# Zero fills in pieces, planes copies on ScalarE, the last row scatters ahead of the meta scatters, and doubled expert operands with a single landing buffer

## The chip, the cores and the metric

One core of a Trainium2 chip. The time is that of one execution of the program on the device, in microseconds (us), as a median of repeated runs. A profiled execution gives the trace.

## What is computed

A transformer block on x of 2048 tokens by 512, all in float32: a linear attention layer with 32 heads of 64, then a mixture of 8 experts of which each token takes 2.

```python
xn = layernorm(x)
q = relu(xn @ Wq); k = relu(xn @ Wk); v = xn @ Wv           # 512 x 2048 each, 32 heads
kv = einsum('bhsd,bhse->bhde', k, v)
out = einsum('bhsd,bhde->bhse', q, kv) / clip(q . k.sum(axis=2), 1e-6)
x = x + out @ Wo + bo
xf = layernorm(x)
scores = xf @ gate_w.T + gate_b + bias
gates = softmax(top_k(scores, 2))
h = silu(w1[e] @ xf + b1[e])                                # 352 wide
x = x + sum over the two experts e of gates * (w2[e] @ h + b2[e])
```

## The kernel before

The program is written engine by engine (SP for DMA issues, GpSimd, ScalarE, VectorE, TensorE), each with its list in program order; semaphores alone order them against each other. A matmul with near-float32 precision is made of three (function `three`): an operand is split into a high part (a cast, ScalarE) and a low part (the rest, VectorE). SBUF is laid out by hand, and many buffers share an address at different times.

**Stage K** (to about 390 us): four column chunks c of Wk, each with 16 row tiles. Chunk 0 also makes layernorm 1 and the transposes of x, and it splits Wk: `load_wk(c)` loads 1 MB into the single buffer wk_in, `split_wk` (ScalarE and VectorE) makes wk_hi and wk_lo. `WK_SPLIT` places these splits in the row tiles of chunk 0: block 1 in tiles 2 to 5, block 2 in tiles 8 to 11, block 3 in tiles 13 to 15. Chunks 1 to 3 take in four head pairs each (`load_pair`, `pe_kv`, `pe_m`), which are loaded when m of two pairs before is put. The SP list ahead of the pairs also holds `zero_rows`: xr_dram, a DRAM scratch of 137 blocks of 128 rows of 2 KB, is filled with zeros, because unused slots of an expert's last tile must read as zeros.

**Stage Q** (to about 805 us): 16 row tiles of four column blocks: project q, normalize, transpose, multiply by m. Then layernorm 2 (xn2), gate scores (`dots`, one VectorE instruction with a product into gprod for each expert), top 2 (`put_scores`). GpSimd routes: `put_mask` makes the mask of a tile from its top 2, TensorE ranks it (`rank`, held by mask_ready), VectorE adds the expert's base (`put_slot8`), `put_slots` makes two slots for each token, `put_rows` scatters the rows of xn2 to them in xr_dram (indirect DMAs, L699) and L714 scatters the token's number and score difference to meta_dram. Rows are scattered as two planes of 16 bits (low words, high words), which the copy `put_planes` (L725, GpSimd) makes in xp. The Q list of ScalarE is `act_unit` and `act_tile`: act_q, act_qsT, act_qs in each block.

**Stage W** (to about 842 us): w1 and w2 come in as raw float32, 46 steps k; TensorE transposes one (`w_transpose`), ScalarE makes the high part (`w_hi`), VectorE the low part (`w_lo`) or, for the steps in PE_STEPS, TensorE and ScalarE (`subtract_hi`, `w_act_lo`). Meanwhile GpSimd puts the last two tiles in slots and makes the table: first half meta_row (which block of xr_dram each expert tile reads), then the last row scatters and the gather of the meta rows (L809), then the second half tile_expert, then the bias columns of experts 6 and 7 (`put_b2`, L768), which w_transpose of steps 40 and on need.

**Expert stage** (to about 1022 us): 39 tiles of 128 slots. `load_tile(i)` (SP, L583) loads 128 rows with a transposing DMA into xgT; ScalarE copies the low words (`act_rec`, L1177) and VectorE the high words (`dve_rec`, L1630) into gx, the record. From gx come gT_hi (ScalarE) and gT_lo (VectorE), then h on TensorE (`pe_h`), a copy of h (ScalarE, h_in), its transposes (`pe_hT`, L2039), silu (ScalarE), hT_hi and hT_lo (VectorE), y (`pe_y`, two tiles behind h), y times the gate (`dve_y`, VectorE, L1648), and the scatter that adds y to out (`add_out`, GpSimd, L763). xgT has two buffers; gx, gT_hi, gT_lo and the PSUM banks of h and y have one each. ScalarE makes record i + 1 ahead of the copy of h of tile i.

Of the kernel before, what the change touches and what calls it, by code (L numbers as in the profile page):

```python
# [48 lines left out]
E = 8  # L49
# [8 lines left out]
MROWS = E * EROWS + 1  # L58
FAR = 1e30
# [5 lines left out]
def block_kernel(nc, x, Wq, Wk, Wv, Wo, bo, gate_w, gate_b, gbias, w1, b1, w2, b2, out):  # L65
    xnT_dram = nc.dram_tensor("xnT_dram", (NT, P, D), F32, kind="Internal").ap()
    xr_dram = nc.dram_tensor("xr_dram", (MROWS * P, 2 * D), U16, kind="Internal").ap()
# [52 lines left out]
    gprod = sb("gprod", D, 201 * KB)  # L120
# [98 lines left out]
    gT_hi = sb("gT_hi", D, 184 * KB, F32R)  # L219
    gT_lo = sb("gT_lo", D, 186 * KB, F32R)  # L220
    gx = sb("gx", D, 188 * KB)
    h_in = sb("h_in", H, 190 * KB)
    hT_hi = [sb("hT_hi0", HB * P, 190 * KB + 1408, F32R), sb("hT_hi1", HB * P, M0 + 5120, F32R)]
    hT_lo = [sb("hT_lo0", HB * P, 190 * KB + 2944, F32R), sb("hT_lo1", HB * P, 190 * KB + 4480, F32R)]
    xgT = [sb(f"xgT{b}", 2 * D, (196 + 2 * b) * KB, U16) for b in range(2)]
    y_last = sb("y_last", D, 198 * KB)
    y = sb("y", 2 * D, M0 + 1024)

    with ExitStack() as ctx:
# [131 lines left out]
        s_xt = [sem(f"s_xt{i}") for i in range(2)]  # L361
# [49 lines left out]
        y_bank = lambda i: pA[:, (i - (NS - 2)) * 512:(i - (NS - 3)) * 512] if isinstance(i, int) and i >= NS - 2 else pK[:, 512:1024]  # L411
        hT = pT[:, 0:HB * P]
        planes = lambda a: a[:, :].rearrange("p (h n) -> p h n", h=2)
        words = lambda a: a[:, :].bitcast(U16).rearrange("p (n h) -> p h n", h=2)

        @block.sync
        def _(sp):
# [29 lines left out]
            sp.dma_start(xr_dram[E * EROWS * P:MROWS * P, :].rearrange("p (h n) -> p h n", h=2),  # L447
                         zero16[:, :].unsqueeze(1).to_broadcast([P, 2, D])).then_inc(xr_zeroed, 16)
            sp.wait_ge(wk_lo_ready, 3 * FB)
            load_wk(3)  # L450
# [123 lines left out]
            sp.wait_ge(s_metain, 16)  # L574
# [3 lines left out]
            def load_tile(i):  # L578
                if i >= 2:
                    sp.wait_ge(rec_lo, i - 1)  # L580
                    sp.wait_ge(rec_hi, i - 1)
                row = sp.value_load(meta_row[i:i + 1, 0:1], min_val=0, max_val=MROWS - 1)
                sp.dma_start_transpose(xgT[i % 2][:, :].rearrange("p (c n) -> p c n", n=P),  # L583
                                       xr_dram[ds(row * P, P), :]).then_inc(s_xt[i % 2], 16)
# [13 lines left out]
        def _(pool):  # L598
# [69 lines left out]
            pool.wait_ge(xr_zeroed, 16 * (E + 1))  # L668
# [25 lines left out]
            def put_rows(r, b):  # L694
                rows = xp_last if isinstance(r, int) and r == NT - 1 else xp
# [151 lines left out]
        def _(act):  # L847
# [354 lines left out]
            def act_tile_e(i, b, e=None, last=False):  # L1202
# [3 lines left out]
                if not last:  # L1206
                    act_gT(i + 1)
# [895 lines left out]
```

## Time and profile before

| | us |
|---|---|
| median of 3 runs | 1029.01 |
| lowest and highest | 1028.38, 1030.11 |
| the profiled execution | 1029.53 |
| its span | 1027.8 |

| engine | busy us | share of the span | instructions |
|---|---|---|---|
| TensorE (PE) | 995.1 | 97% | 4863 |
| VectorE (DVE) | 736.7 | 72% | 1593 |
| ScalarE (ACT) | 543.3 | 53% | 1361 |
| GpSimd (POOL) | 266.3 | 26% | 423 |

The span is the time between the first and the last instruction; the execution takes 1.7 us more. The granted clock of TensorE is 0.99 of full speed as a mean. In the rows a timeline line is: start, length, engine, line of the kernel, operation, output from input, count, and in brackets the idle time of the engine before it and what ended it. A row of the windows is one stretch: its bounds and width, busy us (and instructions) of PE, PEld, DVE, ACT and POOL, the granted clock, the busy share of the DMA engines and what they moved in GB/s. L12 is line 12 of the kernel.

### The profile page before, as it was taken

What the parts mean: (1) busy time and instruction counts of PE and PEld (TensorE: products, weight loads), DVE (VectorE), ACT (ScalarE), POOL (GpSimd) and SP (SyncE); (2) the same over time, 40 slices, a digit from 0 to 9 for tenths busy, and PEclk for the clock granted to TensorE, in tenths of its full rate; (3) what the DMA queues carried; (4) which work ended last, traced back from release to release, by engine and by line L of the source; (5) the groups of instructions that cost most, each with busy time, mean ns of one, the idle gap of its engine ahead of it and who ended that gap; (6) DMA issues with size and microseconds to landing.
All of it is one profiled execution on the core that took longest, in us unless ns stands there. A gap on an engine that the chain in (4) does not pass through costs nothing. (4 is left out here: it accounts for less than half of the span.)

```text
span 1027.8 us, 17481 instructions
## 1 busy us (share of the span) xinstructions
PE 995.1 (97%) x4863; PEld 827.6 (81%) x4864; DVE 736.7 (72%) x1593; ACT 543.3 (53%) x1361; POOL 266.3 (26%) x423
## 2 busy tenths in 40 slices
PE   9998799999999999999899999999999979999998
PEld 7876688888888888888788887888888868888886
DVE  7876565565556567857788888888888866666665
ACT  4542544444444455865455555555555775555553
POOL 1000000000000002222644444444444752333334
PEclk9999899999999999999999999999999989999999
DMA  9999592000010011332211111111115854776873
GB/s 320 374 348 340 183 374 90 21 20 20 20 40 23 20 62 62 103 119 96 90 63 52 51 51 51 53 59 51 59 43 141 234 162 78 118 106 106 117 111 53
DMA packets 120254, 115.20 MB, mean 112 GB/s; under 512 B 47033, under 2 KB 94570, under 8 KB 120082
## 3 DMA queue, kind: packets, MB, share of 16 engines
q1 hardware_dynamic: 110962, 97.73, 31.3%
q0 software_dynamic: 9248, 16.95, 8.7%
q8 instruction: 20, 0.33, 0.1%
q14 instruction: 24, 0.20, 0.1%
HBM read 42.91 MB, written 63.35 MB: 103 GB/s over the span
## 5 line engine op out<-in xcount | busy, mean ns | idle before, releaser
L1013 ACT ACTIVATE qs<-q,nrec 128x64 f32<-128x64 f32 x512 | 129.6, 335 | 106.9 <-DVE nrec L1404 104.2
L621 POOL TENSOR_TENSOR wv_lo<-wv_in,wv_hi 128x512 fp32r<-128x512 f32 x4 | 5.2, 1292 | 417.3 <-ACT wo_hi L934 417.3
L1686 PE MATMUL pK<-wk_hi,xnT_hi 128*128 128x512 f32 (+1 forms) x256 | 101.0, 394 | 11.9 <-DVE xnT_lo L1259 11.8
L1686 PE MATMUL pA<-k_hi,xn_hi 128*128 128x512 f32 x256 | 101.0, 394 | 0.5 <-DVE k_lo L1279 0.5
L1686 PE MATMUL pK<-wq_hi,xnT_hi 128*128 128x512 f32 x256 | 100.5, 393 | 0.0
L1687 PE MATMUL pK<-wk_lo,xnT_hi 128*128 128x512 f32 (+1 forms) x256 | 100.4, 392 | 0.0
L1688 PE MATMUL pK<-wk_hi,xnT_lo 128*128 128x512 f32 (+1 forms) x256 | 100.2, 391 | 0.0
L1688 PE MATMUL pK<-wq_hi,xnT_lo 128*128 128x512 f32 x256 | 99.8, 390 | 0.0
L1688 PE MATMUL pA<-k_hi,xn_lo 128*128 128x512 f32 x256 | 99.8, 390 | 0.0
L1687 PE MATMUL pA<-k_lo,xn_hi 128*128 128x512 f32 x256 | 99.7, 389 | 0.0
L1687 PE MATMUL pK<-wq_lo,xnT_hi 128*128 128x512 f32 x256 | 99.7, 389 | 0.0
L1686 PE MATMUL pX<-m_hi,qsT_hi 128*128 128x512 f32 x240 | 99.6, 415 | 0.0
L1688 PE MATMUL pX<-m_hi,qsT_lo 128*128 128x512 f32 x240 | 94.8, 395 | 0.0
L1687 PE MATMUL pX<-m_lo,qsT_hi 128*128 128x512 f32 x240 | 94.3, 393 | 0.0
L763 POOL DMA_INDIRECT out<-y,slot_token x38 | 59.1, 1556 | 123.5 <-DMA out<-y,slot_token 85.5
L1279 DVE SCALAR_TENSOR_TENSOR k_lo<-pK,k_hi 128x512 fp32r<-128x512 f32 x64 | 44.1, 689 | 57.3 <-ACT k_hi L881 57.3
L875 ACT CAST xn_hi<-xn 128x512 fp32r<-128x512 f32 x64 | 39.8, 621 | 68.6 <-PE pA L1688 68.6
L881 ACT ACTIVATE k_hi<-pK 128x512 fp32r<-128x512 f32 x64 | 38.1, 595 | 68.3 <-PE pK L1688 68.2
L1397 DVE TENSOR_TENSOR qs<-q,ksum 128x512 f32<-128x512 f32 x64 | 44.1, 690 | 38.4 <-ACT q L1007 33.2
L1686 PEld LDWEIGHTS pK<-wk_hi,xnT_hi 128*128 128x128 f32 x256 | 48.5, 189 | 22.7 <-DVE xnT_lo L1259 13.0
L1007 ACT ACTIVATE q<-pK 128x512 f32<-128x512 f32 x64 | 38.2, 597 | 52.1 <-PE pK L1688 50.6
L1259 DVE TENSOR_TENSOR xn_lo<-xn,xn_hi 128x512 fp32r<-128x512 f32 x64 | 44.1, 689 | 27.7 <-ACT xn_hi L875 27.7
(281 smaller groups left out, 2503.0 us busy)
## 6 DMA issues: line engine op xcount, KB each, us to landing
xr_dram<-zero SPq DMA_DIRECT2D x8, 4352.0 KB, 28.8
w_in<-in_ffn_w SPq DMA_DIRECT2D x22, 256.0 KB, 3.2
w_in<-in_ffn_w SPq DMA_DIRECT2D x8, 704.0 KB, 6.1
xn<-in_attn_hidden_states SPq DMA_DIRECT2D x16, 256.0 KB, 6.4
wv_in<-in_attn_Wv SPq DMA_DIRECT2D x16, 256.0 KB, 2.7
wo_in<-in_attn_Wo SPq DMA_DIRECT2D x16, 256.0 KB, 2.9
wk_in<-in_attn_Wq SPq DMA_DIRECT2D x4, 1024.0 KB, 5.7
xnT_dram<-xnT SPq DMA_DIRECT2D x4, 1024.0 KB, 11.7
```

The source lines that it names most:

```text
L621: pool.tensor_tensor(wv_lo[:, b], wv_in[:, b], f(wv_hi[:, b]), ALU.subtract).then_inc(wv_lo_ready, 1)
L763: pool.indirect_dma_start(out, bass.IndirectOffsetOnAxis(slot_token[:, i:i + 1].bitcast(U32), 0), rows, None, bounds_check=T - 1, oob_is_e ...
L875: nc.scalar.copy(xn_hi[:, b * D:(b + 1) * D], xn[:, ds(t * D, D)]).then_inc(xn_hi_ready, 1)
L881: nc.scalar.activation(k_hi[:, b * CW:(b + 1) * CW], pK[:, b * 512:(b + 1) * 512], ACT.Relu).then_inc(k_hi_ready, 1)
L1007: nc.scalar.activation(q[:, b * CW:(b + 1) * CW], pK[:, b * 512:(b + 1) * 512], ACT.Relu).then_inc(q_ready, 1)
L1013: i = nc.scalar.activation(qs[:, s], q[:, s], ACT.Copy, scale=nrec[:, b * HC + h:b * HC + h + 1])
L1259: return nc.vector.tensor_tensor(dst, src, f(hi), ALU.subtract)
L1279: nc.vector.scalar_tensor_tensor(out=k_lo[:, s], in0=pK[:, b * 512:(b + 1) * 512], scalar=0.0, in1=f(k_hi[:, s]), op0=ALU.max, op1=ALU.sub ...
L1397: nc.vector.tensor_tensor(qs[:, b * CW:(b + 1) * CW], q[:, b * CW:(b + 1) * CW], ksum[:, c * CW:(c + 1) * CW], ALU.mult).then_inc(qk_ready, 1)
L1686: nc.tensor.matmul(dst, lhs[0], rhs[0], start=start, stop=False)
L1687: nc.tensor.matmul(dst, lhs[0], rhs[1], start=False, stop=False)
L1688: return nc.tensor.matmul(dst, lhs[1], rhs[0], start=False, stop=stop)
```

## The change

1. xr_dram is rounded up to 140 blocks. The zero fills leave the head of the SP list; ten pieces of 14 blocks stand one behind each `load_pair` of pairs 2 to 11. `load_wk(1)` to `load_wk(3)` follow each other.
2. `put_planes` of tiles 0 to 14 moves from GpSimd to ScalarE (in `act_tile` behind act_qs of block 1), that of tile 15 to VectorE. gprod gets a second buffer.
3. The row scatters of tiles 14 and 15 go with their slots; the meta scatters of these two follow the first half of the table (`put_meta`), and the gather of the meta rows and TensorE's transposes of them come behind put_b2(7) and behind h of tile 0. SP loads w2 of experts 6 and 7 without the wait for the gather, and `load_tile` waits for rows_ready (meta_row) instead of experts_ready.
4. gT_hi, gT_lo, gx, the h bank and the y bank have two buffers each; gx shares its place with gT_lo. xgT has one. Record i + 2 is made behind the copy of h of tile i. Records 0 and 1 are made between weight steps 43 and 45.

```diff
-            def zero_rows(first, last):
-                for e in range(first, last):
-                    sp.dma_start(xr_dram[e * EROWS * P:(e + 1) * EROWS * P, :].rearrange("(p r) (h n) -> p (r h) n", p=P, h=2),
-                                 zero16[:, :].unsqueeze(1).to_broadcast([P, 2 * EROWS, D])).then_inc(xr_zeroed, 16)
-
-            sp.wait_ge(wk_lo_ready, FB)
-            load_wk(1)
-            sp.wait_ge(zero_early, 1)
-            zero_rows(0, 3)
-            sp.wait_ge(wk_lo_ready, 2 * FB)
-            load_wk(2)
-            zero_rows(3, 6)
...
-            sp.wait_ge(wk_lo_ready, 3 * FB)
-            load_wk(3)
+            for c in range(1, NC):
+                sp.wait_ge(wk_lo_ready, c * FB)
+                load_wk(c)
...
-            zero_rows(6, E)
-            sp.wait_ge(xr_zeroed, 16 * (E + 1))
+            sp.wait_ge(zero_early, 1)
 
             with sp.Fori(1, NP // 2 - 2) as h:
                 for b in range(2):
                     sp.wait_ge(m_put, 2 * h + (b - 1))
                     load_pair(2 * h + b, b)
+                    sp.dma_start(xr_dram[ds((2 * h + (b - 2)) * (ZROWS * P), ZROWS * P), :].rearrange("(p r) (h n) -> p (r h) n", p=P, h=2),
+                                 zero16[:, :].unsqueeze(1).to_broadcast([P, 2 * ZROWS, D])).then_inc(xr_zeroed, 16)
...
-            sp.wait_ge(s_metain, 16)
             for e in range(6, E):
                 load_w2(e)
 
             def load_tile(i):
-                if i >= 2:
-                    sp.wait_ge(rec_lo, i - 1)
-                    sp.wait_ge(rec_hi, i - 1)
+                if i >= 1:
+                    sp.wait_ge(rec_lo, i)
+                    sp.wait_ge(rec_hi, i)
...
-            sp.wait_ge(experts_ready, 1)
             sp.wait_ge(s_xr, 32 * (NT - 1))
             sp.wait_ge(s_xr_last, 32)
+            sp.wait_ge(rows_ready, 1)
...
+            def put_meta(b):
+                for c in range(2):
+                    pool.indirect_dma_start(meta_dram, bass.IndirectOffsetOnAxis(slot_i[b][:, c:c + 1].bitcast(U32), 0),
+                                            vals[b][:, 2 * c:2 * c + 2], None).then_inc(s_meta[b], 16)
...
+                put_rows(r, b)
                 if not isinstance(r, int) or r < NT - 2:
-                    put_rows(r, b)
...
+                    put_meta(b)
...
-            put_rows(NT - 2, 0)
+            pool.tensor_scalar(meta_row[:, :].unsqueeze(1), row8[:, :, 0:1], float(MROWS - 1), None, ALU.min).then_inc(rows_ready, 1)
             for b in range(2):
-                pool.wait_ge(s_meta[b], 16 * NT)
-            pool.indirect_dma_start(meta_in[:, :], None, meta_rows, bass.IndirectOffsetOnAxis(meta_row[:, :].bitcast(U32), 0)
-                                    ).then_inc(s_metain, 16)
-            put_rows(NT - 1, 1)
+                put_meta(b)
...
+            def put_planes(t):
+                act.wait_ge(xn2_ready, t + 1)
+                if isinstance(t, int) and t == NT - 2:
+                    act.wait_ge(dots_done, E * t)
+                elif not (isinstance(t, int) and t == 0):
+                    act.wait_ge(s_xr, 32 * t)
+                to = xp_last if isinstance(t, int) and t == NT - 2 else xp
+                nc.scalar.copy(planes(to), words(xn2[:, :])).then_inc(xp_ready, 1)
...
                     act_qs(m, c % 2)
+                    if c == 1:
+                        put_planes(t - 2)
...
+            def act_expert(i, b):
+                act_h(i, b)
+                if not isinstance(i, int) or i + 2 < NS:
+                    act_rec(i + 2, b)
+                    act_gT(i + 2, b)
+                act_silu(i)
...
-            with dve.Fori(2, NS // 2) as h:
+            with dve.Fori(2, (NS - 3) // 2) as h:
                 for b in range(2):
-                    dve_rec(2 * h + (b + 1), 1 - b)
-                    dve_gT(2 * h + (b + 1))
+                    dve_rec(2 * h + (b + 2), b)
+                    dve_gT(2 * h + (b + 2), b)
                     dve_y(2 * h + (b - 2), b, 16 * h - 16)
                     dve_hT(2 * h + b, b)
...
             pe.wait_ge(experts_ready, 1)
-            first_expert = expert(0)
-            pe.wait_ge(w_lo_ready, len(DVE_STEPS) - 2)
-            pe.wait_ge(w_act_ready, len(PE_STEPS))
-            pe_h(0, first_expert)
+            pe_h(0, 0, expert(0))
+            meta_transpose()
+            pe_h(1, 1, expert(1))
             pe_hT(0)
-            pe_h(1, expert(1))
-            pe.wait_ge(w_lo_ready, len(DVE_STEPS))
             pe_hT(1)
```

## Rows read from the trace of the kernel before

**Rows 1.** Windows: the expert stage (columns as told above).

```profile
858.00:1018.00 160.00, 159.49 (x856) 138.82 (x855) 108.63 (x177) 91.42 (x211) 56.05 (x36) 1.00 0.71 105
```

**Rows 2.** Timeline of TensorE behind the first hole, and a window after it.

```profile
109.64 0.79 PE L1686 MATMUL pK<-wk_hi,xnT_hi 128*128 128x512 f32 x1 [10.86 <-DVE xnT_lo L1259]
...
110.00:115.00 5.00, 5.00 (x16) 3.95 (x16) 2.64 (x6) 1.59 (x4) 0.00 (x0) 0.69 0.00 0
```

**Rows 3.** Waits: who waited for whom, total us, times, longest us.

```profile
ACT wk_hi L854 <- DMA wk_in<-in_attn_Wk: 12.5, 1, 12.5
...
SPq L457 <- PE pX L1688: 208.6, 11, 22.5
```

**Rows 4.** Timeline of the SP queue in stage K.

```profile
13.26 30.00 SPq L437 DMA_DIRECT2D xr_dram<-zero  x3
...
96.10 1.38 SPq L419 DMA_DIRECT2D wk_in<-in_attn_Wk  x1
```

**Rows 5.** Timeline of GpSimd and TensorE near 500 us.

```profile
497.99 1.04 POOL L725 COPY xp<-xn 128x1024 uint16<-128x1024 uint16 x1
...
501.10 0.17 PE L1912 MATMUL pT<-mask,before 128*128 128x8 bf16 x1 [2.52 <-issue]
```

**Rows 6.** Timeline of GpSimd and TensorE in stage W.

```profile
825.37 1.10 POOL L699 DMA_INDIRECT xr_dram<-xp,slot_i  x1 [0.82 <-POOL meta_row L805]
...
831.41 0.31 PE L2014 MATMUL pX<-ident,meta_in 40*128 40x40 f32 x1 [1.26 <-DMA meta_in<-meta_dram,meta_row]
...
831.60 0.76 POOL L813 TENSOR_TENSOR cmp<-iota_j,small 128x320 f32<-128x320 f32 x1
...
835.61 0.32 POOL L768 COPY w_in<-b2T 128x4 f32<-128x4 f32 x2
...
836.54 1.15 PE L1954 MATMUL pA<-ident,w_in 128*128 128x128 f32 x8
```

**Rows 7.** Chain of work that ended last: h transposes of tiles 2 and 37.

```profile
856.39 0.33 PE pX L2039 x3
...
1013.33 0.33 PE pX L2039 x3
```

**Rows 8.** The page's DMA issues: count, KB each, median us from issue to landing.

```profile
wk_in<-in_attn_Wq SPq DMA_DIRECT2D x4, 1024.0 KB, 5.7
```

**Rows 9.** Timeline of ScalarE, GpSimd and VectorE in a Q tile's third block.

```profile
763.54 0.60 ACT L1007 ACTIVATE q<-pK 128x512 f32<-128x512 f32 x1
...
766.03 1.29 POOL L641 TENSOR_TENSOR xb<-x_in,bo_b 128x512 f32<-128x512 f32 x1 [0.28 <-POOL vals L692]
...
766.16 1.18 DVE L1402 TENSOR_SCALAR nrm<-nrm 128x8 f32<-128x8 f32 x1
```

**Rows 10.** Timeline of records and transposing loads, at the start and in the loop.

```profile
840.16 0.82 ACT L1177 COPY gx<-xgT 128x512 uint16<-128x512 uint16 x1
...
841.66 1.23 SPq L583 DMA_TRANSPOSE xgT<-xr_dram  x1
...
891.50 1.45 SPq L583 DMA_TRANSPOSE xgT<-xr_dram  x1
...
894.85 0.69 DVE L1630 COPY gx<-xgT 128x512 uint16<-128x512 uint16 x1
...
896.27 1.49 SPq L583 DMA_TRANSPOSE xgT<-xr_dram  x1
```

**Rows 11.** Windows of half a microsecond behind two of these loads.

```profile
844.50:845.00 0.50, 0.50 (x4) 0.50 (x3) 0.00 (x0) 0.17 (x1) 0.00 (x0) 0.50 0.04 16
...
895.00:895.50 0.50, 0.50 (x4) 0.41 (x3) 0.50 (x1) 0.19 (x1) 0.50 (x1) 1.00 0.06 12
```

**Rows 12.** Timeline of y and its scatter in the expert loop.

```profile
889.47 1.55 POOL L763 DMA_INDIRECT out<-y,slot_token  x1 [2.66 <-DMA out<-y,slot_token]
...
896.93 0.75 DVE L1648 TENSOR_SCALAR y<-pK,slot_gate 128x512 f32<-128x512 f32 x1
898.46 1.55 POOL L763 DMA_INDIRECT out<-y,slot_token  x1 [2.68 <-DMA out<-y,slot_token]
```

More of the change, by code:

```diff
@@ L217, in block_kernel @@
     gate_e = sb("gate_e", TW, M0 + 7840)
[L219 to L227, printed above, removed]
+    gT_hi = [sb(f"gT_hi{b}", D, (184 + 4 * b) * KB, F32R) for b in range(2)]
+    gT_lo = [sb(f"gT_lo{b}", D, (186 + 4 * b) * KB, F32R) for b in range(2)]
+    gx = [sb(f"gx{b}", D, (186 + 4 * b) * KB) for b in range(2)]
+    h_in = sb("h_in", H, 192 * KB)
+    hT_hi = [sb("hT_hi0", HB * P, 192 * KB + 1408, F32R), sb("hT_hi1", HB * P, M0 + 5120, F32R)]
+    hT_lo = [sb("hT_lo0", HB * P, 192 * KB + 2944, F32R), sb("hT_lo1", HB * P, 192 * KB + 4480, F32R)]
+    xgT = sb("xgT", 2 * D, M0 + 1024, U16)
+    y = [sb("y0", D, 198 * KB), sb("y1", D, M0 + 3072)]
+    y_last = sb("y_last", D, 188 * KB)
     with ExitStack() as ctx:
@@ L360, in block_kernel @@
         hT_ones = sem("hT_ones")
-        s_xt = [sem(f"s_xt{i}") for i in range(2)]
+        s_xt = sem("s_xt")
+        rows_ready = sem("rows_ready")
         rec_lo = sem("rec_lo")
@@ L694, in put_rows @@
             def put_rows(r, b):
-                rows = xp_last if isinstance(r, int) and r == NT - 1 else xp
+                rows = xp_last if isinstance(r, int) and r == NT - 2 else xp
                 pool.wait_ge(xp_ready, r + 1)
@@ L1164, in _ @@
             w_act_lo(3)
-            for k in range(6, WSTEPS - 2):
+            for k in range(6, 43):
                 w_hi(k)
@@ L1195, in act_silu @@
                     act.wait_ge(hT_lo_ready, i)
-                for b in range(HB):
-                    w = min(P, H - b * P)
-                    last = nc.scalar.activation(hT[0:w, b * P:(b + 1) * P], pX[0:w, b * P:(b + 1) * P], ACT.Silu,
-                                                bias=b1T[0:w, ds(b * E + e, 1)])
+                for n in range(HB):
+                    w = min(P, H - n * P)
+                    last = nc.scalar.activation(hT[0:w, n * P:(n + 1) * P], pX[0:w, n * P:(n + 1) * P], ACT.Silu,
+                                                bias=b1T[0:w, ds(n * E + e, 1)])
@@ L1223, in _ @@
                 for b in range(2):
-                    act_tile_e(2 * h + b, b)
-            act_tile_e(NS - 1, 0, last=True)
+                    act_expert(2 * h + b, b)
+            for i in range(NS - 3, NS):
+                act_expert(i, i % 2)
         @block.vector
@@ L2020, in _, with pe_h @@
                     subtract_hi(k - 2)
-                if k == 35:
-                    meta_transpose()
-            def pe_h(i, e):
+            def pe_h(i, b, e):
                 pe.wait_ge(gT_lo_ready, i + 1)
-                if not (isinstance(i, int) and i < 1):
-                    pe.wait_ge(h_ready, i)
+                if isinstance(i, int) and i < 2:
+                    pe.wait_ge(w_lo_ready, DVE_STEPS.index(44 if i else 42) + 1)
+                else:
+                    pe.wait_ge(h_ready, i - 1)
                 for n in range(FB):
-                    last = three(pK[:, 0:H], two((gT_hi, gT_lo), n * P, P), two((w1_hi, w1_lo), e * H + n * EH, H),
+                    last = three(h_bank[b], two((gT_hi[b], gT_lo[b]), n * P, P), two((w1_hi, w1_lo), e * H + n * EH, H),
                                  n == 0, n == FB - 1)
@@ L2034, in pe_hT @@
                 pe.wait_ge(h_ready, i + 1)
-                if not (isinstance(i, int) and i < 1):
+                if isinstance(i, int) and i == 0:
+                    pe.wait_ge(far_ready, 1)
+                else:
                     pe.wait_ge(hT_ready, i)
@@ L2049, in pe_y @@
                     at_ = e * (HB * D) + n * D
[L2050 removed]
+                    last = three(y_bank[b], hs, (w2_hi[0:w, ds(at_, D)], w2_lo[0:w, ds(at_, D)]),
                                  n == 0, n == HB - 1)
```

201 lines of the change are left out of this document (100 added, 101 removed).

## The prediction

> **What bounds the kernel now.** I read the busy time by stage first: TensorE has no hole in the expert stage, where it is busy 159.49 of 160 us [rows 1], and hardly one through the K and Q stages, so an edit there gains nothing unless it shortens TensorE's own work, and this one doesn't. It stands in four places: near 100 us, near 500 us, between 828 and 856 us, and in the tail. I asked of each hole what ended it. The first is the largest: a matmul of 109.64 us comes after 10.86 us of idle time [rows 2]. It waited for VectorE, VectorE for ScalarE, and ScalarE 12.5 us for a Wk load [rows 3]. The SP queue shows why the load is late: it is issued at 96.10 us, behind zero-filling DMAs of which the first three alone hold the queue for 30.00 us [rows 4], and four more follow. In the second hole TensorE's rank matmul of row tile 1 is held 2.52 us; it needs the expert mask that GpSimd makes, and GpSimd had first run the planes copy of 1.04 us [rows 5]. In the third TensorE waits 1.26 us for the gathered meta rows, then for weights and for the first tiles [rows 6]. In the expert stage a tile takes (1013.33 - 856.39) / 35 = 4.484 us from its h transposes to the next tile's [rows 7].
>
> **The change part by part.** The profiled execution is 1029.53 us (span 1027.8 and 1.7 us around it), 0.52 us over the median of 1029.01. The sum is made against 1029.53.
>
> **Zeroing.** No zero DMA stands ahead of the Wk loads any more. Load 3 is then issued when block 2 of Wk is split and needed two row tiles later, which is some 11 us (24 matmuls of 0.23 us each). A load of the same 1 MB lands in 5.7 us where the queue is quiet [rows 8], so it is hidden; if it weren't, what it is late by would come back as a hole. The 10.86 us go. The granted clock had fallen in the hole: 0.69 on average from 110 to 115 us [rows 2], so TensorE lost 0.31 x 5 = 1.55 us there, and half of the 0.36 us from 109.64 to 110. Gain 10.86 + 1.55 + 0.18 = 12.6 us. The ten new pieces of 3.5 MB stand each behind a pair's loads. Three fills of 4.25 MB took 30.00 us, so a piece takes about 8.2 us; SP waits up to 22.5 us between pairs [rows 3, 4]. Each piece is out before the next load is issued: cost nothing, and at most 8.2 us a pair if that cover were gone.
>
> **Planes on ScalarE.** GpSimd loses sixteen copies of 1.04 us. One was on the path: the mask of row tile 1 comes 1.04 us sooner. Bounds: nothing, if ScalarE's new copy holds up qs there, and the whole 2.52 us. I take 1.0 us. ScalarE gains fifteen copies. No row shows one there; half of the words (512 of 1024) takes it 0.82 us [rows 10], so 1.04 (GpSimd's own) to 1.64 us, say 1.2. It is put behind qs of the second column block, where ScalarE goes straight on to the next q at 763.54 us [rows 9]. That q now ends 1.2 us later, at 765.3. VectorE's two reductions of it follow and slip by about 0.6 us. But behind them its short clip (L1402) takes 1.18 us, until 767.34, and GpSimd's xb ends at 767.32 [rows 9]: what releases it doesn't move, so the slip is swallowed. Cost nothing; if the cover is gone, 0.6 us in 13 tiles, 8 us. The Trainium skill ("SBUF — State Buffer", two separate sides) says that VectorE and GpSimd share one port pair as an exclusive lock. By that rule the slip is free and the removed GpSimd copies shorten VectorE's work elsewhere too, where nothing waits for it. The last planes copy goes to VectorE, ahead of weight work that ScalarE paces: nothing. The second gprod takes a semaphore's turn out of the dots, which TensorE doesn't wait for: nothing.
>
> **Row scatters ahead, meta gather late.** TensorE's 1.26 us wait for the gather goes, and VectorE's behind it. What is late next is GpSimd. Between the table's first half and its second it issues five indirect DMAs now (825.37 to 831.60), four then, so the bias columns of experts 6 and 7 come 1.25 us sooner, at about 834.4 instead of 835.61 [rows 6]. Weight step 40 needs them; TensorE makes it at 836.54 [rows 6]. Without the stall it can be there before them, so steps 40 to 45 come 2.1 us sooner. Tile 0 is fetched long before, and its record is made beside step 43, at about 838 us, where it ends at 840.98 now (840.16 + 0.82) [rows 10]. Record 1 must wait for its own load, which can't start before record 0 has been read. Carried forward in turns of 4.5 us (below), records end at 838, 842.5, 847 and 851.5, and h of tile 3 starts some 2.4 us behind record 3, at 853.9; now it starts at 856.7 [rows 7]. Gain 2.5 us, bounds nothing (the ring starts that much later) and 5.
>
> **The expert operands.** gT, gx and the h bank are doubled, and gain nothing where TensorE has no hole [rows 1]. But xgT, where the transposing load lands, becomes single: the load of a tile waits for the records of the tile before, where it waited for those of the one before that. That closes a ring: record ends, SP issues, the load lands, ScalarE makes the record. Its terms: 0.73 us from record to issue (894.85 + 0.69 to 896.27) [rows 10]. From issue to landing: the load issued at 841.66 has left the DMA engines silent by 844.5, the one issued at 891.50, beside a scatter of y, just after 895 [rows 10, 11]; so 2.75 and 3.65 us, and I add 0.25 us until an engine starts on it, an estimate from the width of these windows. ScalarE's record is 0.82 us [rows 10]. Alone the turn is 0.73 + 2.75 + 0.25 + 0.82 = 4.55 us, TensorE's own pace; beside a scatter it is 5.45 us.
>
> Which one? VectorE takes up y behind gT, 1.4 us after the record's end (895.54 to 896.93). y takes 0.75 us, GpSimd starts 0.78 after it and issues for 1.55 [rows 12]; the bytes move some 0.5 us later for about 2.2, both estimates (in the half-microsecond windows, share times width is 1.3 us for the load alone and 3.5 for both). So a scatter ends 7.2 us after a record, 6.5 us after that turn's issue, and 6.5 - T after the next issue, T being the turn. Now the scatter issued at 889.47 ends at 893.7, which is 2.2 us after the issue of 891.50. If the landing moves as the scatter's end does, T = 5.45 + (6.5 - T) - 2.2, so T = 4.87 us; tiles that scatter few rows pull the mean down, and I take 4.8. The ends are 4.55 and 5.45. Over the 34 tiles behind h(3), 34 x (4.80 - 4.484) = 10.7 us is given back.
>
> **Sum.** 1029.5 - 12.6 - 1.0 - 2.5 + 10.7 = 1024.1, less 0.5 for the median: **1023.6 us**.
>
> **The rivals.** (a) The ring doesn't bind and the pace stays 4.484. For it: alone the turn is hardly over that pace, and some tiles scatter few rows. Against: a scatter is under way near almost every load. It gives 1029.5 - 16.1 - 0.5 = 1012.9 us. The Trainium skill ("DMA: Bandwidth & Descriptors", anatomy of one DMA) gives a DMA about 2.0 us plus its bytes over 436 GB/s, an estimate of 2.6 us for 256 KB. By that the turn would be 4.40 us and (a) would hold; the rows have 2.75 and 3.65. (b) The ring binds in full: scatter and load meet in every tile and the turn is 5.45 us, 34 x 0.97 = 33 us given back, 1046 us. It decides for slower above 4.484 + 16.1 / 34 = 4.96 us a turn. For it: the meeting is there now. Against: a longer turn moves the scatter out of the load's way. (c) The first hole stays, because the load is late for another reason and the change doesn't do what it says: 1023.6 + 12.6 = 1036 us. Against: nothing else stands ahead on the queue. (d) The planes on ScalarE cost their 8 us: 1031.6 us.
>
> **How the numbers follow.** The forecast, turns of 4.65 to 4.95 us, 1018 to 1028.5 us: 0.42. (a) 0.27. (b), anything above 4.96: 0.17. (c) 0.05. (d) 0.09. A measurement of this kernel can tell about 0.2% from no change: faster is below 1027.0, slower above 1031.1. Faster: 0.35 of the forecast's 0.42, (a), and 0.03 of (d), 0.65. Within: 0.07 and 0.04 of (d), 0.11. Slower: (b), (c) and 0.02 of (d), 0.24. The range leaves out the slower parts of (b) and (c) and the quickest of (a): 1011 to 1033 us.
>
> **What would show it.** TensorE without a hole at 98 us and at the full clock to 120 us. A wait of about 1.5 us at the rank matmul of row tile 1, and no new idle time of TensorE between 510 and 800 us. No wait for meta; h(3) 2.5 us nearer to the end of the Q stage. In the expert stage each load issued 0.73 us behind a record, ScalarE's record waiting for the DMA of xgT (it never does now), TensorE waiting for gT_lo, and the h transposes 4.8 us apart. A pace of 4.48 proves the ring wrong; a TensorE that waits for qs in every tile proves the free slip wrong. The forecast goes wrong above all if the landing beside a scatter is nearer to one of its two ends than I took it.

## The result, and the profile after

| | before | after |
|---|---|---|
| median of 9 runs, us | 1028.38 | 1032.09 |
| lowest and highest | 1026.78, 1031.34 | 1031.26, 1034.77 |
| span of the profiled execution | 1027.8 | 1029.7 |

The ratio is 1.0033, with a 95% interval of 1.0021 to 1.0045: slower by 0.33%, where a faster kernel, 1023.6 us, was forecast. The time lies inside the range of 1011 to 1033 us, the direction is wrong.

I compare the traces at events that both kernels have: the rank matmul of row tile 0, that of row tile 13 (the end of the Q stage), the start of h of tile 3, and the last instruction.

| event | before | after | ahead by |
|---|---|---|---|
| rank matmul, row tile 0 | 485.87 | 472.00 | 13.9 |
| rank matmul, row tile 1 | 501.10 | 486.04 | 15.1 |
| rank matmul, row tile 13 | 793.99 | 772.12 | 21.9 |
| h of tile 3 | 856.72 | 834.51 | 22.2 |
| end of the span | 1027.8 | 1029.7 | -1.9 |

So the kernel after arrives at its experts 22.2 us sooner, 6.1 us more than forecast, and then gives back 24.1 us where 10.7 were forecast. 13.4 - 6.1 = 7.3 us is what the forecast missed by these traces (7.4 by the profiled executions, 1024.1 against 1031.54). That the time lies inside the range at all is luck: a gain that was not forecast hides nearly half of the miss at the experts.

The first row is the stretch of the old first hole [rows 2], the second the expert stage, to be held against [rows 1], the third the first tiles of the experts (bounds, width, busy us of PE, PEld, DVE, ACT and POOL, granted clock, DMA share, GB/s), all of the kernel after.

```profile
90.00:120.00 30.00, 29.97 (x139) 24.75 (x138) 22.76 (x42) 15.75 (x30) 0.00 (x0) 1.00 0.51 181
...
858.00:1018.00 160.00, 144.92 (x743) 121.47 (x742) 90.79 (x157) 81.13 (x188) 49.42 (x32) 0.99 0.58 93
...
815.00:835.00 20.00, 13.59 (x59) 11.99 (x60) 9.64 (x22) 9.70 (x21) 3.46 (x10) 0.83 0.33 54
```

The hole at 100 us is gone and the granted clock is full there. TensorE, which had no idle time in the expert stage, is idle for 15 of 160 us, and in the first tiles for 6.4 of 20 us, with the granted clock at 0.83. These are waits of the expert loop (840 to 1000 us, after: who waited for whom, total us, times, longest):

```profile
ACT gx L1173 <- DMA xgT<-xr_dram: 63.6, 31, 2.9
DVE gx L1628 <- DMA xgT<-xr_dram: 36.6, 30, 1.8
...
PEld pK L1691 <- issue: 17.0, 19, 1.3
```

No engine waited for xgT before. Now ScalarE does in every tile, 2.05 us each. TensorE's own waits are put down to "issue" (nothing that the profile shows), so what they were for is read from the chain of work. It is the ring that the prediction drew: load, record, SyncE, load (after: start, us, what; a line of the load is its whole way from issue to landing, and the lines left out are of 0.02 to 0.05 us).

```profile
878.87 3.13 DMA xgT<-xr_dram
...
882.02 0.78 ACT gx L1173
...
882.82 1.01 SPq L574
...
883.86 0.15 SPq L574
...
884.21 3.25 DMA xgT<-xr_dram
```

The link that stands out against the forecast is the line of 1.01 us: SyncE reads the row number of the next tile into a register. The same instruction in the loop of either kernel (before, then after: count, ns min/median/max, first and last start):

```profile
L582 SPq TENSOR_LOAD <-meta_row x31: 267/276/287, 863.7 to 998.8; - x31
```

```profile
L574 SPq TENSOR_LOAD <-meta_row x28: 270/659/1045, 851.6 to 992.0; - x28
```

And GpSimd's list beside the chain shows with what it goes (after):

```profile
880.58 1.54 POOL L743 DMA_INDIRECT out<-y,slot_token  x1 [3.41 <-DMA out<-y,slot_token]
885.67 1.54 POOL L743 DMA_INDIRECT out<-y,slot_token  x1 [3.54 <-DMA out<-y,slot_token]
```

The load of the register that starts at 882.82 ends at 883.83, which is 3.25 us after the start of this scatter's issue. The next one (0.62 us, from 888.29) ends at 888.92, again 3.25 us after 885.67. Over the 30 turns from 845 to 1000 us, 21 of these reads took more than 0.4 us, and 17 of the 21 ended 3.17 to 3.25 us after the start of a scatter's issue. The other 9 took 0.27 to 0.29 us and ended before that.

### The profile page after: what moved, and what is told of

It reads as the page before. It is cut to its first block, busy times and chain, and to the rows that moved or that the text cites. A ratio compares the mean times of both kernels' runs of the same rounds, so it can differ in the third digit from the quotient of the medians.

```text
span 1029.7 us, 17472 instructions
## 1 busy us (share of the span) xinstructions
PE 994.1 (97%) x4863; PEld 827.3 (80%) x4864; DVE 709.4 (69%) x1594; ACT 555.8 (54%) x1376; POOL 247.8 (24%) x407
## 4 chain that ended last, share of the span: by engine, by line
PE 76%; DMA 11%; ACT 4%; issue 2%; SPq 2%; POOL 2%; DVE 2%; ACTq 0%; POOLq 0%; DVEq 0%
PE pK L1691 12%; PE pK L1693 12%; PE pK L1692 12%; DMA xgT<-xr_dram 10%; PE pA L1691 7%; PE pA L1693 7%; PE pA L1692 7%; PE pX L1691 5%; PE pX L1693 5%; PE pX L1692 5%; PE pA L1825 3%; ACT gx L1173 2%; SPq L574 2%; PE pT L1771 2%; PE pT L1706 1%
## 5 line engine op out<-in xcount | busy, mean ns | idle before, releaser
L1393 DVE TENSOR_TENSOR qs<-q,ksum 128x512 f32<-128x512 f32 x64 | 52.2, 815 | 55.3 <-ACT q L989 55.3
L1173 ACT COPY gx<-xgT 128x512 uint16<-128x512 uint16 x39 | 30.5, 783 | 76.7 <-DMA xgT<-xr_dram 76.7
```

What stands on the lines that cost most here:

```text
L1173: nc.scalar.copy(words(gx[b][:, :])[:, 0, :], planes(xgT)[:, 0, :]).then_inc(rec_lo, 1)
L1393: nc.vector.tensor_tensor(qs[:, b * CW:(b + 1) * CW], q[:, b * CW:(b + 1) * CW], ksum[:, c * CW:(c + 1) * CW], ALU.mult).then_inc(qk_ready, 1)
```

## The experiments

In each, the ratio is that of the kernel to the kernel before, on the same chip, with its 95% interval. The chips differ from run to run (the kernel before had a median of 1028.72 us beside e1 to e4, 1030.04 beside e5 to e8 and 1030.37 beside e9), so where 1 or 2 us decide, ratios are compared and not times. Four terms of the ring, read from the timelines between 845 and 1000 us (870 and 1030 in e6) as means over some 30 turns, carry most verdicts:

| kernel | issue of the load to start of ScalarE's record | the record | its end to the next issue | turn |
|---|---|---|---|---|
| the forecast | 3.25 | 0.82 | 0.73 | 4.80 |
| after | 3.41 | 0.78 | 1.05 | 5.24 |
| e1, early register load | 4.11 | 0.78 | 0.12 | 5.02 |
| e3, narrow scatter | 3.27 | 0.78 | 0.70 | 4.75 |
| e6, before with one xgT | 3.51 | 0.78 | 1.03 | 5.32 |

To compare with a loop that has no ring I take another mean, the pace of TensorE from its h transposes of tile 2 to those of tile 37: 4.48 us a tile before, 5.16 after, 5.01 in e1, 4.38 in e2, 4.78 in e3 and 5.28 in e6.

**e2: is the ring the whole loss?** xgT is doubled again and the rest of the expert stage stays double. The memory comes from h_in, which moves into gT_hi of its own tile:

```diff
-    h_in = sb("h_in", H, 192 * KB)
-    xgT = sb("xgT", 2 * D, M0 + 1024, U16)
+    h_in = [sb(f"h_in{b}", H, (184 + 4 * b) * KB) for b in range(2)]
+    xgT = [sb("xgT0", 2 * D, M0 + 512, U16), sb("xgT1", 2 * D, M0 + 4608, U16)]
...
-                if i >= 1:
-                    sp.wait_ge(rec_lo, i)
-                    sp.wait_ge(rec_hi, i)
+                if i >= 2:
+                    sp.wait_ge(rec_lo, i - 1)
+                    sp.wait_ge(rec_hi, i - 1)
...
+            sp.wait_ge(w_sub_put, len(PE_STEPS))
             for i in range(NS):
...
                 act_rec(i + 2, b)
-                act_gT(i + 2, b)
                 act_silu(i)
+                act_gT(i + 2, b)
```

> The changed kernel with xgT doubled again, as in the kernel before, and all else of the expert stage left double: h_in goes into the memory of gT_hi of its own tile, so the next gT_hi is written behind the silu. Theory A (the ring is the whole of what the expert loop lost): the ring is cut, the turn falls from 5.23 to the 4.3 to 4.5 us that TensorE's work takes, 34 turns give back 25 to 31 us, 1001 to 1007. Rival B (the loop is slower for another reason, such as the order of the waits on VectorE): above 1020.

Measured: 1004.18 us, ratio 0.9750 (0.9723 to 0.9778), some 28 us faster than the kernel after. The windows row of its loop and h transposes in its chain of work:

```profile
858.00:980.00 122.00, 121.36 (x670) 108.40 (x669) 79.21 (x140) 69.32 (x166) 45.86 (x28) 1.00 0.76 113
```

```profile
891.53 0.33 PE pX L2050 x3
...
895.85 0.33 PE pX L2050 x3
...
900.15 0.33 PE pX L2050 x3
...
904.46 0.33 PE pX L2050 x3
```

TensorE has no hole, and these three tiles take it (904.46 - 891.53) / 3 = 4.31 us each; the mean from tile 2 to tile 37 is 4.38. Against it the kernel after loses 5.16 - 4.38 = 0.78 us a tile, 27 us in 35 tiles, of the 28 us between the two kernels. One thing keeps this from settling rival B by itself: the shared memory of h_in also asks for another order, hT ahead of gT on VectorE and the silu ahead of gT on ScalarE, and rival B named the order on VectorE. e6 below changes nothing but xgT. e2 also shows something that the prediction had at nothing: the loop takes 4.484 - 4.38 = 0.10 us a tile less than in the kernel before, where TensorE's own row in the windows had looked full [rows 1]. The doubled gT, gx and banks are the likely cause; no run takes them apart from the new order.

**e6: the ring alone.** The kernel before, with one xgT and nothing else:

```diff
-    xgT = [sb(f"xgT{b}", 2 * D, (196 + 2 * b) * KB, U16) for b in range(2)]
+    xgT = [sb("xgT", 2 * D, 196 * KB, U16)] * 2
...
-                if i >= 2:
-                    sp.wait_ge(rec_lo, i - 1)
-                    sp.wait_ge(rec_hi, i - 1)
+                if i >= 1:
+                    sp.wait_ge(rec_lo, i)
+                    sp.wait_ge(rec_hi, i)
```

> The kernel before with xgT single and nothing else: the load of a tile waits for both records of the tile before. Theory A (the ring of one xgT is enough to lose the time, whatever the other operands do): a turn of 5.0 to 5.25 us, as in the kernel after, instead of 4.48 in some 36 turns, so 19 to 28 us slower than before, 1048 to 1057. Rival F (the doubled operands and banks are part of the loss, for example by the order in which VectorE serves them): under 10 us slower, below 1038.

Measured: 1057.86 us, ratio 1.0272 (1.0244 to 1.0300): 28 us slower, just above the range that theory A gave. Its chain shows the same links with the same sizes, the long register load among them:

```profile
899.98 3.31 DMA xgT<-xr_dram
903.29 0.02 issue
903.31 0.79 ACT gx L1177
904.10 0.02 issue
904.12 0.84 SPq L582
...
905.34 3.11 DMA xgT<-xr_dram
```

In the kernel before, this register load took 276 ns at the median. Only the moment at which it runs has changed. There it started 1.4 us behind the start of a scatter's issue and was over by 1.7 us (rows of 886 to 914 us); in the ring it starts 1.8 to 2.8 us behind one in most turns. The longest reads start 2.2 us behind. Rival F falls, and with it what was left of rival B: the ring alone makes the whole loss.

**e1: the register load taken off the ring.**

```diff
+                row = sp.value_load(meta_row[i:i + 1, 0:1], min_val=0, max_val=MROWS - 1)
                 if i >= 1:
                     sp.wait_ge(rec_lo, i)
                     sp.wait_ge(rec_hi, i)
-                row = sp.value_load(meta_row[i:i + 1, 0:1], min_val=0, max_val=MROWS - 1)
```

> The changed kernel with one thing moved: SyncE reads the row number of the next tile into a register before it waits for the records of the tile before, not after. Theory A (the ring of the single xgT sets the pace, and SyncE's register load, 483 ns at the median in the profile after, is one of its links): a turn goes from 5.23 to about 4.75 us, 34 turns give back 16 us, about 1016. Rival B (the pace is set by something else in the loop, TensorE's own stream or the scatters, and the waits for xgT only show who comes last): within 2 us of 1032.

Measured: 1024.03 us, ratio 0.9949 (0.9932 to 0.9966), so some 8 us faster than after, half of what was expected. The turn is 5.02 and not 4.75 us. Chain and GpSimd's timeline of e1:

```profile
880.26 4.08 DMA xgT<-xr_dram
...
884.37 0.80 ACT gx L1173
...
885.18 0.05 SPq L575
...
885.27 4.12 DMA xgT<-xr_dram
```

```profile
877.93 1.54 POOL L743 DMA_INDIRECT out<-y,slot_token  x1 [3.42 <-DMA out<-y,slot_token]
883.02 1.54 POOL L743 DMA_INDIRECT out<-y,slot_token  x1 [3.54 <-DMA out<-y,slot_token]
```

The issue now follows the record in 0.12 us, but the load takes 4.1 us. It starts 2.33 us behind the scatter's issue of 877.93 (the next one 2.25 us behind 883.02); in the kernel after it started 3.63 us behind (880.58 to 884.21) and took 3.25 us. So the two links stand in for each other: either the register load or the transfer is long beside a scatter, and 0.93 us saved at the one comes back as 0.70 us at the other. The turns of the kernel after show the same by themselves: behind the 17 reads that ended 3.2 us after a scatter's issue the load took 3.0 to 3.3 us, and behind the 9 short ones 3.2 to 4.3. Neither theory had that. The ring stays the bound (rival B, no gain, falls), but its turn can't be had from terms that are sized one by one.

**e3: the ring without the scatters' bytes.** The expert outputs are not added to out: 64 bytes a row go to a scratch tensor.

```diff
-                pool.indirect_dma_start(out, bass.IndirectOffsetOnAxis(slot_token[:, i:i + 1].bitcast(U32), 0),
-                                        rows, None, bounds_check=T - 1, oob_is_err=False,
-                                        compute_op=ALU.add).then_inc(s_add[i % 2], 16)
+                pool.indirect_dma_start(narrow, bass.IndirectOffsetOnAxis(slot_token[:, i:i + 1].bitcast(U32), 0),
+                                        rows[:, 0:16], None, bounds_check=T - 1, oob_is_err=False).then_inc(s_add[i % 2], 16)
```

> The changed kernel, but the expert outputs are not added to out: each scatter writes 64 bytes a row to a scratch tensor, with no read of what is there. Theory A with the scatter in two of its links (the transfer that lands beside it and SyncE's register load that is slowed when it starts): landing falls from 3.3 to about 3.0 us at the median and the register load to 0.27 us, so a turn is about 4.7 us and the time about 1014. Rival C (the register load is slow for a reason of its own and landing is 3.3 us anyway): 1029 to 1032.

Measured: 1015.78 us, ratio 0.9862 (0.9835 to 0.9888), a turn of 4.75 us. Both links shrink, the one behind the record from 1.05 to 0.70 us and the load from 3.41 to 3.27 us. The scatter is still issued at its place, so what lengthens the two links is what it moves (the width of its rows or the add, of which e3 takes out both), and not its issue. The run also sizes the ring's other part: with these narrow scatters a tile still takes 4.78 us, more than the 4.38 us of e2. Of the 0.78 us lost a tile, the wide scatters with add cause 0.38 and the ring by itself 0.40.

**e5: the zeroing alone.** The kernel before, with the ten pieces between the pair loads and nothing ahead of the Wk loads (part 1 of the change).

```diff
-            zero_rows(6, E)
-            sp.wait_ge(xr_zeroed, 16 * (E + 1))
+            sp.wait_ge(zero_early, 1)
...
                     load_pair(2 * h + b, b)
+                    sp.dma_start(xr_dram[ds((2 * h + (b - 2)) * (ZROWS * P), ZROWS * P), :].rearrange("(p r) (h n) -> p (r h) n", p=P, h=2),
+                                 zero16[:, :].unsqueeze(1).to_broadcast([P, 2 * ZROWS, D])).then_inc(xr_zeroed, 16)
```

> The kernel before with the zeroing alone changed: ten pieces between the pair loads, nothing ahead of the Wk loads. The profile after is 14.4 us ahead at the first expert projection of the Q stage, of which my sum had 12.6. If the zeroing is the whole of that: 12.6 to 14.4 us faster than before, 1014 to 1016. If part of it came from elsewhere, or is given back in the Q stage and at the experts: 1018 or more.

Measured: 1015.78 us, ratio 0.9876 (0.9853 to 0.9900), a gain of 12.8 us by the ratio (10 to 15 by its interval). In the profiles the rank matmul of row tile 0 is 14.3 us ahead, that of row tile 2 16.5 and the end of the span 15.1. The gain is kept through the experts, since the expert stage is the old one. The 2.1 us between row tiles 1 and 2 have a cause of their own, told next.

**e4 and e7: where 6.8 us came from in the Q stage.** Between the rank matmuls of row tiles 1 and 13 the kernel after gained 6.8 us for which the sum had nothing: 2.16 us between row tiles 1 and 2, and 4.65 us in the eleven row tiles behind them. Beside the zeroing, which e5 has alone, two edits touch that stage. e4 takes the kernel after and gives GpSimd its planes copies back (row tiles 0 to 13); e7 takes e2 and gives it one gprod again.

```diff
+            def put_planes(t):
+                pool.wait_ge(xn2_ready, t + 1)
+                if not (isinstance(t, int) and t == 0):
+                    pool.wait_ge(s_xr, 32 * t)
+                pool.nop(nofuse=True)
+                pool.tensor_copy(planes(xp), words(xn2[:, :])).then_inc(xp_ready, 1)
...
                 for b in range(2):
+                    put_planes(2 * h + (b - 2))
                     put_mask(2 * h + (b - 2), b, 32 * h - 32)
...
-                    if c == 1:
-                        put_planes(t - 2)
```

> The changed kernel with the planes of rows 0 to 13 made by GpSimd again, ahead of the mask as in the kernel before; the last two stay with ScalarE and VectorE. The profile after is 14.4 us ahead at 403 us and 21.9 us ahead at 772 us, so 7.5 us were gained in the Q stage in steps of 0.3 to 0.6 us a row tile. Theory D (the planes on GpSimd cost them, by holding up VectorE and so the qs that TensorE transposes): 5 to 8 us slower than the changed kernel, 1037 to 1040. Rival E (they came from the other edits of that stage: gprod doubled, metas behind the rows, the zeroing gone): within 1.5 us of 1032.

```diff
-    gprod = [sb("gprod0", D, 201 * KB), sb("gprod1", D, 198 * KB)]
+    gprod = sb("gprod", D, 201 * KB)
...
-                        dve.wait_ge(dots_done, E * t + (e - 1 - E))
+                        dve.wait_ge(dots_done, E * t + (e - E))
```

> The kernel of e2_two_xgT with one gprod again, as in the kernel before: each dot of VectorE waits until the one before it is done. The row tiles of the Q stage take about 23.85 us in the profile after and 24.25 in the one before, also where GpSimd makes the planes in both. Theory G (the second gprod is what shortened them): 3.5 to 4.5 us slower than e2_two_xgT, 1008, and a row tile at 24.1 or more. Rival H (it does nothing, as the prediction said, and another edit did it): 1004, a row tile at 23.85.

Measured: e4 1036.78 us, ratio 1.0070 (1.0047 to 1.0092), e7 1002.60 us, ratio 0.9735 (0.9718 to 0.9753), not slower than e2. The start of the rank matmul of some row tiles, and the pace between tiles 4 and 11:

| kernel | planes by | gprod | tile 0 | tile 2 | tile 4 | tile 11 | us a tile |
|---|---|---|---|---|---|---|---|
| before | GpSimd | one | 485.87 | 527.05 | 575.68 | 745.89 | 24.32 |
| e5 | GpSimd | one | 471.53 | 510.57 | 559.26 | 729.47 | 24.32 |
| e4 | GpSimd | two | 473.12 | 515.39 | 563.14 | 729.92 | 23.83 |
| e7 | ScalarE | one | 472.18 | 509.72 | 557.39 | 724.21 | 23.83 |
| after | ScalarE | two | 472.00 | 509.83 | 557.52 | 724.40 | 23.84 |

Either edit alone brings the pace down by 0.49 us a tile, and both together bring no more. So neither theory D nor G nor their rivals were right: it is an or. (The time of e4 alone, 1036.78 us, would have looked like theory D.) The groups of dots with gate weights in gw_late show the load on VectorE (group, count, busy us, mean ns, idle before), for 600 to 700 us of before, and for 590 to 690 of e4, e7 and after, in this order:

```profile
L1440 DVE SCALAR_TENSOR_TENSOR gprod<-xn,gw_late 128x512 f32<-128x512 f32 x4 | 8.8, 2201 | 0.1
```

```profile
L1445 DVE SCALAR_TENSOR_TENSOR gprod<-xn,gw_late 128x512 f32<-128x512 f32 x4 | 7.8, 1959 | 0.0
```

```profile
L1439 DVE SCALAR_TENSOR_TENSOR gprod<-xn,gw_late 128x512 f32<-128x512 f32 x5 | 3.5, 691 | 0.2
```

```profile
L1438 DVE SCALAR_TENSOR_TENSOR gprod<-xn,gw_late 128x512 f32<-128x512 f32 x5 | 3.5, 706 | 0.0
```

Where GpSimd copies the planes, one dot of VectorE in each row tile takes 2.0 to 2.2 us instead of 0.7. And that was on TensorE's path, by a wait which I had not looked up. The waits of the kernel before, 600 to 700 us:

```profile
ACT qs L1013 <- DVE nrec L1404: 31.2, 17, 2.9
...
PEld pA L1820 <- ACT qs L1013: 3.3, 8, 0.6
```

TensorE's weight load of the qs transposes waits 0.4 us for ScalarE's qs, twice a row tile; ScalarE waits for VectorE's reciprocal. In 100 us of the kernel after, of e4 and of e7 these waits come to 0.4 or 0.5 us in all, and in e5 to the same 3.3. In e4 the dot is long as before and TensorE doesn't wait for it: with the second gprod the stretch of dots seems to have the slack that takes it up. That is argued from these rows, no run shows it alone.

What e4 still loses against the kernel after is 1.1 us at row tile 0, for which I have no row, 1.5 us at row tile 1, where the rank matmul waits 3.19 us (2.52 before [rows 5]), and 3.0 us between row tiles 1 and 2. That last part is TensorE's clock, and so is most of the 2.16 us there by which the kernel before is behind the kernel after. The windows of 8 us behind the wait of row tile 1, of before, after, e5, e3, e8 and e4, in this order:

```profile
500.00:508.00 8.00, 6.91 (x25) 5.60 (x26) 4.66 (x14) 2.02 (x8) 5.62 (x14) 0.79 0.11 39
```

```profile
486.00:494.00 8.00, 8.00 (x41) 6.65 (x40) 6.27 (x17) 4.21 (x12) 4.66 (x11) 1.00 0.11 37
```

```profile
486.00:494.00 8.00, 7.24 (x36) 6.05 (x37) 5.06 (x15) 3.39 (x11) 5.62 (x14) 1.00 0.17 60
```

```profile
486.00:494.00 8.00, 8.00 (x35) 6.46 (x35) 4.88 (x14) 3.02 (x11) 4.53 (x11) 0.79 0.19 33
```

```profile
486.00:494.00 8.00, 8.00 (x35) 6.44 (x34) 4.86 (x14) 3.02 (x11) 4.64 (x12) 0.79 0.08 31
```

```profile
486.00:494.00 8.00, 5.35 (x15) 4.22 (x16) 5.29 (x15) 2.10 (x9) 5.74 (x15) 0.62 0.17 33
```

A mean clock of 0.79 over 8 us costs 0.21 x 8 = 1.7 us, one of 0.62 costs 3.0. Behind a wait of 2.53 us e5 kept the full clock, where the kernel before lost it behind 2.52. e3 and e8 have the code of the kernel after up to this point and the same wait of 1.8 us, and they lost it. So these 1.7 us come or not with the execution, and no run shows what decides it. They belong to neither edit, and a comparison of single profiles has to leave them out.

**e8 and e9: what can still be had.** e8 puts the bias columns of experts 6 and 7 ahead of the second half of the table, in the kernel of e2.

```diff
                 put_meta(b)
+            pool.wait_ge(w_put, W1T)
+            pool.wait_ge(w_sub_put, W1_SUBS)
+            put_b2(6)
+            put_b2(7)
...
-            pool.wait_ge(w_put, W1T)
-            pool.wait_ge(w_sub_put, W1_SUBS)
-            put_b2(6)
-            put_b2(7)
```

> The kernel of e2_two_xgT with the bias columns of experts 6 and 7 put ahead of the second half of the table, where they stood behind it. TensorE waits 1.27 us for them at weight step 40 in the profile after. If that wait is on the path: 1.0 to 1.3 us faster than e2_two_xgT, 1003, and no wait at step 40. If the first tiles' gT_lo waits take it over (h of tile 0 waits 2.2 us for its own operand): no change in time, 1004, and a longer wait at h of tile 0.

Measured: 1005.59 us, ratio 0.9760 (0.9742 to 0.9779) against 0.9750 for e2: no gain. Its profile holds the 1.7 us of clock near 490 us that e2's doesn't. In the profile of e2 TensorE doesn't wait for these columns. It waits 5.0 us for tile 0, and so it does in e8 (5.08), because I had placed xgT0 over neg_ident and made the first load wait for the last subtraction. The experiment asked its question of a kernel in which another wait covered the answer, so it says nothing of the 1.27 us in the kernel after. e9 removes that cover: the kernel of e7 with the two xgT buffers exchanged, so that only the second load waits.

```diff
-    xgT = [sb("xgT0", 2 * D, M0 + 512, U16), sb("xgT1", 2 * D, M0 + 4608, U16)]
+    xgT = [sb("xgT0", 2 * D, M0 + 4608, U16), sb("xgT1", 2 * D, M0 + 512, U16)]
...
+            load_tile(0)
             sp.wait_ge(w_sub_put, len(PE_STEPS))
-            for i in range(NS):
+            for i in range(1, NS):
```

> The kernel of e7_two_gprod1 with the two xgT buffers exchanged, so that the load of tile 0 goes to memory that is free early and doesn't wait for the last subtraction of weight stage W. In the profile of e2_two_xgT that load is issued at 812.6 us and TensorE waits 5.0 us for gT_lo of tile 0, where the kernel after issued it at 803.8 and waited 2.2 us. Theory (the late first load is the difference): the wait falls to about 2.2 us and the time by 2.5 to 3 us against e7_two_gprod1, 999.5 to 1000. Rival (the record waits for the memory of the last weights anyway, and the load is not what is late): no change, 1002.5.

Measured: 1000.16 us, ratio 0.9710 (0.9692 to 0.9729), the best of the study: 30 us under the kernel before and 32 under the kernel after. That is 2.4 us under e7, where the theory gave 2.5 to 3. It was the late load that held up tile 0: TensorE now waits 2.24 us for it as in the kernel after, and for the columns ahead of it again:

```profile
811.97 1.06 PE L1962 MATMUL pA<-ident,w_in 128*128 128x128 f32 x8 [1.28 <-POOL w_in L750]
...
817.02 0.42 PE L1694 MATMUL pK<-w_hi,gT_hi 128*128 x1 [2.24 <-DVE gT_lo L1259]
```

## Why the prediction was wrong

The ring turned the direction: it took 24.1 us where 10.7 were forecast. The other misses are smaller and pull both ways.

**The zeroing** (12.6 us): right. The kernel after is 13.9 us ahead at row tile 0 of the ranks, e5 gains 12.8 us in the time. The lead at 120 us is 14.4 us, of which 12.8 came with the hole and the clock behind it, and 0.6 went again between 400 and 430 us. Some 1.4 us of the lead are older than the hole: the kernel before waits for an earlier Wk load too (waits of the kernel before, 55 to 75 us), and TensorE is idle for 0.93 us at 68.41 behind that; I passed over it.

```profile
ACT wk_hi L854 <- DMA wk_in<-in_attn_Wk: 2.7, 1, 2.7
```

**Planes on ScalarE.** The copy takes ScalarE 1.03 us, where 1.2 were taken. The 1.0 us at row tile 1 came as 1.2 us, and TensorE waits 1.84 us there for qs instead of 2.52 us for the mask (timeline of the kernel after):

```profile
485.51 0.66 PE L1825 MATMUL pA<-ident,qs 128*128 128x128 f32 x4 [1.84 <-ACT qs L995]
```

That the slip of q is swallowed was right: there is no new idle time of TensorE from 510 to 800 us, rival (d) is out. The step that failed is "the removed GpSimd copies shorten VectorE's work elsewhere too, where nothing waits for it", and with it "the second gprod takes a semaphore's turn out of the dots, which TensorE doesn't wait for: nothing". TensorE did wait, for qs, by way of ScalarE; 4.65 us were to be had, and the sum had nothing for them. The other 2.16 of the 6.8 us came behind row tile 1, where the clock stayed full in this execution; that part is luck. The sign of it was in the list of waits of the weight loads, which I didn't read because the stage is busy 99.5 of 100 us: a wait of 0.4 us between pipelined matmuls hardly shows as idle time. The Trainium skill ("SBUF — State Buffer", two separate sides) says that VectorE and GpSimd share a port pair as an exclusive lock. The trace agrees that the two don't run side by side at full speed: in the kernel before a dot of 611.56 to 613.75 us lies around a copy of 612.15 to 613.20. It has its 2.2 us instead of 0.7, but 1.5 us more is longer than the copy of 1.04, so the copy alone doesn't give the size. I had cited the rule and priced its result at nothing.

**Stage W** (2.5 us): 0.3 us came. Step 40 is at 812.17 against 836.54, 24.4 us ahead, 2.5 more than at the end of the Q stage, where 2.1 were forecast. It is lost again in the first tiles (timeline of the kernel after, then a window of it, then the one of the kernel before at the same work, h of tile 2):

```profile
812.17 1.07 PE L1959 MATMUL pA<-ident,w_in 128*128 128x128 f32 x8 [1.27 <-POOL w_in L748]
...
817.22 0.42 PE L1691 MATMUL pK<-w_hi,gT_hi 128*128 x1 [2.24 <-DVE gT_lo L1255]
...
822.14 0.43 PE L1691 MATMUL pA<-w_hi,gT_hi 128*128 x1 [2.37 <-DVE gT_lo L1255]
...
827.74 0.55 PE L2046 MATMUL pX<-ident,h_in 128*128 128x128 f32 x3 [1.52 <-ACT h_in L1184]
```

```profile
829.00:833.00 4.00, 4.00 (x16) 3.72 (x15) 2.37 (x5) 2.69 (x6) 0.00 (x0) 0.57 0.51 37
```

```profile
852.00:856.00 4.00, 4.00 (x20) 3.49 (x21) 2.18 (x4) 1.86 (x4) 0.00 (x0) 1.00 0.33 74
```

The step that failed here is "h of tile 3 starts some 2.4 us behind record 3". The records themselves came as forecast: put back by the 21.9 us of lead, ScalarE's end at 837.4, 842.4, 846.9 and 851.7 us, where 838, 842.5, 847 and 851.5 stood. But h of tile 3 starts 4.7 us behind the end of record 3 (829.84 to 834.51), and in the kernel before it was 3.9 (852.88 to 856.73): TensorE is still at h of tile 2 and y of tile 0. These take it from 828.59 to 834.26, 5.7 us with the clock at 0.57 in the row above, against 4.3 us at the full clock in the kernel before (851.97 to 856.24). So 1.4 of the 2.2 us that were lost behind step 40 are the clock, which fell behind the waits shown; the rest is these waits.

**The ring** (10.7 us given back): the mechanism was right, and it is the whole loss (e2, e6). The size was wrong. The forecast's turn was 4.80 us; it is 5.24 (5.16 by TensorE's pace over all tiles), above the 4.96 us at which by the prediction it decides for slower. Of its terms the load was nearly right (3.25 against 3.41 us), and so was the record (0.82 against 0.78). The step that failed is "0.73 us from record to issue", which is 1.05: I took it from one row of a kernel in which SyncE reads its register early enough behind a scatter's issue to be done in 0.28 us. The 0.73 us is the undisturbed value; e3 has 0.70. The second error is that of the form: T = 5.45 + (6.5 - T) - 2.2 lets a longer turn move the scatter out of the load's way. But y, and with it the scatter, hangs on the same ring, so it comes back at nearly the same place in each turn, and the load or the register load pays for it (e1). This is rival (b), which I gave 0.17, at a turn between the forecast's and its 5.45.

Rival (a) is out. The Trainium skill ("DMA: Bandwidth & Descriptors", anatomy of one DMA) has its 2.0 us and bytes over 436 GB/s as a fit to DMAs that GpSimd issues; put on this load of SyncE it makes an estimate of 2.6 us. The trace doesn't agree: the transposing load takes 3.0 us at the least, 3.2 at the median and 4.3 at the most (xgT in the kernel after, 845 to 1000 us).

```profile
DMA to landing us min/median/max: 3.0/3.2/4.3
```

Rival (c) is out as well. In all: 22.2 us came sooner instead of 16.1, 24.1 went instead of 10.7. One more term was missing on the other side: with two landing buffers the new loop is 0.10 us a tile faster than the old one (e2), some 4 us, which one landing buffer of 2 KB hid. The prediction had said that nothing is to be had in a stage where TensorE is busy 159.49 of 160 us.

## What to carry to other kernels

A buffer that is made single puts everything between its reader's end and its next fill on one ring: size the turn from rows in which its neighbours run at the phase that the ring itself will give them, and ask which of them it drags along, for these come back in every turn. A stage that is 99% busy can still lose 2% of its time to waits of the weight loads; read their waits too before an edit there is costed at nothing. And two edits can free the same slack, so take each out alone and in the other's absence before one of them gets the credit. Last, look up the granted clock before a step of a microsecond or two between two profiles is given to an edit.

## What the runs showed of the hardware

SyncE's read of one word of SBUF into a register took 270 ns to 1.05 us, and in 17 of the 21 turns where it was long it ended 3.17 to 3.25 us after the start of a scatter's issue on GpSimd (after, 845 to 1000 us). In e3, where the scatters move 64 bytes a row, it took 266 to 283 ns in every turn. That it stands behind the scatter's traffic in some queue is what this suggests; no run shows which.

The transposing load took 3.25 us when it was issued 3.63 us behind a scatter's issue (after) and 4.1 us when issued 2.3 us behind one (e1); single turns of e1 at that distance had 3.2 us. VectorE's dot of 128 x 512 took 2.2 us beside a GpSimd copy of 1.04 us and 0.7 us without.

TensorE's granted clock fell behind a wait of 1.8 us in two executions (e3, e8) and stayed full behind the same wait in others (after, e2). It fell behind one of 2.52 us in the kernel before and stayed full behind one of 2.53 us in e5.
